# Summing the nine product planes of an image: one strided tensor_reduce in place of four additions

## The chip, the cores and the metric

The kernel runs on one core of one Trainium2 chip. The metric is the device time of one execution in microseconds (us). Three timed runs of the kernel before gave 154.48, 154.02 and 157.14 us, so their median is 154.48 us. All data are fp32.

## The reference, cut to what matters

The input x is 8 images of 32 channels of 128 x 128 points. Two layers follow each other. The first scales and filters each image with a 3 x 3 filter per group of channels, whose nine taps come from the mean of the image through a small matrix, a normalisation and a tanh. The second takes a 2-D Hartley transform, keeps 20 x 20 modes, mixes the channels of each mode with a weight matrix, transforms back, blurs over the images, the channels, the rows and the columns, and sets the columns of high frequency to zero.

```python
lf = tanh(bn(x.mean((2, 3)) @ conv_w.T))            # nine taps per image and group
low = sum(shifted(x, t) * lf[t] for t in range(9))  # reflect padding at the edges
x = (low * (inside + 1) - inside * gap) * lamb_l + x * (lamb_h + 1)
x_ht = dht_2d(x)
out_ht[:, :, :20, :20] = compl_mul2d(x_ht[:, :, :20, :20], w1)
y = gaussian_smoothing_4d(dht_2d(out_ht) / (H * W)) * mask
```

The kernel never filters the full image. It transforms the raw image first and applies the filter to the kept modes: each mode of the filtered image is a sum of nine products (the real and imaginary part of the mode times a coefficient, four for the edge rows and three for the edge columns). That sum of nine is what the change touches.

## The kernel before, in words

**First part, image by image (n = 0 to 7).** SyncE loads an image in four pieces. TensorE transforms the rows of each piece (`stage1(n, g)`, L370), VectorE transposes the result out of PSUM in two halves (`turn_y(n, 0)` and `turn_y(n, 1)`, L715), TensorE transforms the other axis (`stage2(n)`, L385), VectorE transposes that into the tile `data` (`turn_data(n)`, L724). TensorE then computes the filter logits from `data` (`filter_logits`, L399), ScalarE makes the taps (`taps(n)`, L607 and L612), TensorE spreads them (`pick_taps`, L405) and ScalarE copies them (L618), and TensorE multiplies them with a table into coefficients in PSUM (`coefficients(n)`, L418).

**The combination on VectorE, one per image m.** `combine_products(m)` (L736 to L748) multiplies data and coefficients: planes 0 to 5 of the tile `terms`, and a small tile `prod_a`. `combine_edges(m)` sums `prod_a` with a tensor_reduce (L756, 144 elements to 18 per partition) and writes planes 6 to 8 of `terms` (L758). `combine_sum(m)` adds the nine planes of 126 elements per partition (L767 to L773) and writes `parts` (L780), the sums and differences of mode pairs. Each of these steps waits by the semaphore `f_step` for the one before it on the same engine.

**The order on VectorE** is written out by hand. In the pass for n (2 to 7) it is: `combine_products(n - 2)`, `turn_y(n, 0)`, `turn_data(n - 1)`, `combine_edges(n - 2)`, `combine_sum(n - 2)`, `turn_y(n, 1)`. In the pass for n = 7 one more instruction, `share_early` (L787, semaphore `last_share`), comes between `combine_sum(5)` and `turn_y(7, 1)`. After the passes come the combinations of images 6 and 7.

**The order on TensorE** in the same pass: `stage1(n, 0)`, `coefficients(n - 2)`, `stage1(n, 1)`, `stage2(n - 1)`, `stage1(n, 2)`, `filter_logits(n - 1)`, `stage1(n, 3)`, `pick_taps(n - 1)`. `stage2(n - 1)` needs both halves of `turn_y(n - 1, ...)`.

**Behind the passes.** GpSimd blurs over the images as the `parts` come (L897 to L902, tile `acc`). For output images 0 and 1, ScalarE lays `acc` out as the operand `mixin_a` (L590, L630) once `last_share` is there; only then it makes the taps of images 6 and 7, for which TensorE waits. TensorE mixes channels for these two (`mix_early`, L444) between `coefficients(6)`, `stage2(7)`, `filter_logits(7)` and `coefficients(7)`. GpSimd and VectorE lay out `mixin_b` for the other six images (L590, L905), which `mix_late` needs.

**Second part, image by image.** TensorE runs `turn` (L496), `to_columns` (L514) and `to_rows` (L532); ScalarE and VectorE copy between them out of PSUM (L563, L650, L834, L569). SyncE stores the rows of an image in three pieces (L346) as they become ready.

Of the kernel before, what the change touches and what calls it, by code (L numbers as in the profile page):

```python
# [8 lines left out]
MODES = 20  # L9
GROUPS, TAPS = 8, 9  # L10
J, Q, S = 4, 3, 2
# [8 lines left out]
NB1 = MODES + 1  # L20
WIDE = SQ * NB1
ND, NA, NB = 2 * WIDE, 3 * SQ * 8, 4 * WIDE
NTAB = ND + NA + NB
NTERM = 9
# [154 lines left out]
def hartley_conv_kernel(nc, x, wide, taps_table, params, conv_wt, mix_w, out):  # L179
    fp32 = mybir.dt.float32  # L180
    ALU = mybir.AluOpType
    ACT = mybir.ActivationFunctionType
    AX = mybir.AxisListType
# [5 lines left out]
    def view(ap, *dims):  # L189

        return bass.AP(tensor=ap.tensor, offset=ap.offset, ap=[ap.ap[0], *[list(d) for d in dims]])
# [6 lines left out]
    with ctx:  # L198
        def sb(name, shape):
            return ctx.enter_context(nc.sbuf_tensor(name, shape, fp32))  # L200

        def sem(name):
# [15 lines left out]
        prod_a = sb("prod_a", [128, 3 * SQ, 8])  # L218
        coef_a = sb("coef_a", [128, 3 * SQ])
        terms = sb("terms", [128, NTERM, WIDE])  # L220
        parts = sb("parts", [128, 2, 2, Q * MODES])
        spread = sb("spread", [128, N, PLANE])
        acc = sb("acc", [128, N, PLANE])
# [19 lines left out]
        coef_done, coef_used, f_step, parts_done, spread_done, acc_done, last_share = map(  # L243
            sem, ("coef_done", "coef_used", "f_step", "parts_done", "spread_done", "acc_done", "last_share"))
# [10 lines left out]
        B_T, B_F = 3, (5, 6, 7)  # L255
        B_IDLE = 3
        B_TURN, B_MIX_A, B_MIX_B = 1, 0, (0, 7, 0)
        F_LINKS = 7
        WPART = S * Q * MODES // 8

        def const(offset, *dims):
# [425 lines left out]
        def _(dve):  # L687
            tt, tr = nc.vector.tensor_tensor, nc.vector.tensor_reduce
# [63 lines left out]
            def combine_edges(m):  # L752

                base = m * F_LINKS
                dve.wait_ge(f_step, base + 1)
# [5 lines left out]
            def combine_sum(m):  # L761

                base = m * F_LINKS
                flat = lambda plane, count: view(terms[:, plane, 0:1], (1, count * WIDE))
                dve.wait_ge(coef_used, m + 1)
                dve.wait_ge(f_step, base + 3)
                tt(flat(0, 4), flat(0, 4), flat(4, 4), ALU.add).then_inc(f_step, 1)  # L767
                dve.wait_ge(f_step, base + 4)
                tt(flat(0, 2), flat(0, 2), flat(2, 2), ALU.add).then_inc(f_step, 1)
                dve.wait_ge(f_step, base + 5)  # L770
                tt(flat(0, 1), flat(0, 1), flat(1, 1), ALU.add).then_inc(f_step, 1)
                dve.wait_ge(f_step, base + 6)
                tt(flat(0, 1), flat(0, 1), flat(8, 1), ALU.add).then_inc(f_step, 1)  # L773
                dve.wait_ge(f_step, base + 7)
                if m >= 2:
                    dve.wait_ge(acc_done, m - 1)
                low = view(terms[:, 0, 0:1], (NB1, Q), (1, MODES))
                high = view(terms[:, 0, Q * NB1 + MODES:Q * NB1 + MODES + 1], (NB1, Q), (-1, MODES))
                for part, op in ((0, ALU.subtract), (1, ALU.add)):
                    last = tt(view(parts[:, m % 2, part, 0:1], (MODES, Q), (1, MODES)), low, high, op)  # L780
                last.then_inc(parts_done, 1)
# [12 lines left out]
            for n in range(1, N):  # L794
                if n >= 2:
                    combine_products(n - 2)
                turn_y(n, 0)
                turn_data(n - 1)
                if n == 2:
                    dve.wait_ge(basis_in, 16)  # L800
                if n >= 2:
                    combine_edges(n - 2)
                    combine_sum(n - 2)
                if n == N - 1:
                    share_early()
                turn_y(n, 1)
# [5 lines left out]
            last.then_inc(gaps_zero, 1)  # L812
            combine_edges(N - 2)
            combine_sum(N - 2)
            combine_products(N - 1)
            combine_edges(N - 1)
            combine_sum(N - 1)

            dve.wait_ge(parts_done, N)
# [151 lines left out]
```

## Time and profile before

| | us |
|---|---|
| median of three runs | 154.48 |
| the profiled execution: its own time | 155.25 |
| its span, first to last instruction | 153.4 |
| TensorE busy | 132.0 (86%) |
| VectorE busy | 84.7 (55%) |
| GpSimd busy | 55.1 (36%) |
| ScalarE busy | 34.0 (22%) |
| mean granted TensorE clock, share of full speed | 0.929 |

A row of the profile names the line of the kernel, the engine, the operation, the tile written and the tile read, and the shape as partitions x elements per partition. An idle time stands with what ended it, its releaser. The time around the span (155.25 less 153.4, so 1.85 us) is not resolved in the trace. Busy shares are averages over stages that have different limits, so a stage has to be read by itself.

### The profile page before, as it was taken

The page shows a single profiled execution, that of the slowest core. Times are in us where ns is not written, and L with a number is a line of the kernel's source. Part 1 is how long each engine was busy: PE and PEld are TensorE (multiplying, and loading weights), DVE is VectorE, ACT ScalarE, POOL GpSimd, SP SyncE. Part 2 cuts the span into 40 slices and gives each one's busy share as a digit, 9 for nine tenths or more (in the row PEclk, how much of TensorE's full clock was granted, in tenths as well). Part 3 has the DMA queues.
Part 4 walks back from the last instruction along what each step waited for, and adds up shares of the span by engine and source line. Part 5 has one row for each costly group of instructions (what it writes and reads, how often), then busy time and mean ns, then how long its engine had stood idle before and what let it go on. Part 6 is the DMA issues. An engine that isn't in the chain of part 4 may idle for free.

```text
span 153.4 us, 5617 instructions
## 1 busy us (share of the span) xinstructions
PE 132.0 (86%) x2508; PEld 76.8 (50%) x2508; DVE 84.7 (55%) x188; ACT 34.0 (22%) x86; POOL 55.1 (36%) x40
## 2 busy tenths in 40 slices
PE   6656999999999999950999999889999999999700
PEld 4322454545454545420566856745785766746200
DVE  0033347899989898993028994045536345454400
ACT  3000310202020202008003353123334342343300
POOL 8999400040737281919999571000000000000000
PEclk9995599999999999996559999999999999999985
DMA  4999999999999997000000006906955988989993
GB/s 145 310 238 299 353 351 355 366 365 366 365 351 361 349 349 230 0 0 0 4 4 4 6 4 218 326 12 222 328 210 196 364 301 284 383 287 386 378 385 140
DMA packets 35456, 36.79 MB, mean 240 GB/s; under 512 B 1156, under 2 KB 35284, under 8 KB 35432
## 3 DMA queue, kind: packets, MB, share of 16 engines
q1 hardware_dynamic: 35432, 36.43, 71.8%
q8 instruction: 20, 0.33, 0.9%
q14 instruction: 4, 0.03, 0.1%
HBM read 19.65 MB, written 16.78 MB: 238 GB/s over the span
## 4 chain that ended last, share of the span: by engine, by line
PE 78%; DMA 6%; DVE 4%; SPq 3%; ACT 2%; issue 2%; ACTq 0%; DVEq 0%
PE ps L532 19%; PE ps L370 18%; PE ps L385 11%; PE ps L514 8%; PE ps L496 7%; DMA x_ring<-x 6%; PE ps L418 6%; PE ps L444 5%; PE ps L405 1%; SPq L312 1%; ACT mixin_a L590 1%; PE ps L357 1%; PE ps L399 1%; DVE rows L569 1%; DVE data L724 1%
## 5 line engine op out<-in xcount | busy, mean ns | idle before, releaser
L370 PE MATMUL ps<-x_ring,k_wide 64*64 64x256 f32 x512 | 38.5, 426 | 4.5 <-DMA x_ring<-x 4.5
L532 PE MATMUL ps<-cols,k_wide 128*64 128x330 f32 (+1 forms) x192 | 31.4, 467 | 0.1
L370 PEld LDWEIGHTS ps<-x_ring,k_wide 64*64 64x64 f32 x512 | 18.4, 145 | 20.8 <-issue 11.0
L715 DVE STREAM_TRANSPOSE y_sb<-ps 128x1024 f32<-128x1024 f32 x16 | 19.9, 1242 | 15.6 <-PE ps L370 15.6
L532 PEld LDWEIGHTS ps<-cols,k_wide 128*64 128x64 f32 x192 | 12.7, 136 | 13.5 <-issue 5.4
L569 DVE COPY rows<-ps 128x330 f32<-128x330 f32 (+1 forms) x24 | 12.6, 525 | 10.2 <-PE ps L532 9.4
L385 PE MATMUL ps<-y_sb,k_wide 128*32 128x256 f32 x256 | 17.1, 411 | 0.0
L900 POOL TENSOR_TENSOR spread<-parts,k_wide 128x960 f32<-128x960 f32 (+1 forms) x5 | 8.6, 1728 | 18.8 <-DVE parts L780 18.8
L569 ACT COPY rows<-ps 128x330 f32<-128x330 f32 (+1 forms) x24 | 11.1, 462 | 18.0 <-PE ps L532 18.0
L514 PEld LDWEIGHTS ps<-k_wide,modes 64*64 64x64 f32 x384 | 11.8, 134 | 3.9 <-issue 3.6
L514 PE MATMUL ps<-k_wide,modes 64*64 64x66 f32 x384 | 12.9, 220 | 0.0
L385 PEld LDWEIGHTS ps<-y_sb,k_wide 128*32 128x32 f32 x256 | 8.4, 118 | 7.8 <-issue 4.1
L607 ACT ACTIVATE tap_tanh<-ps,bn 72x1 f32<-72x1 f32 x8 | 2.8, 348 | 42.3 <-PE ps L399 42.3
L902 POOL TENSOR_TENSOR acc<-acc,spread 128x960 f32<-128x960 f32 (+1 forms) x5 | 10.7, 2132 | 0.4
L496 PE MATMUL ps<-k_wide,mixed 96*32 96x96 f32 (+2 forms) x512 | 10.5, 233 | 0.0
L496 PEld LDWEIGHTS ps<-k_wide,mixed 96*32 96x32 f32 x512 | 9.7, 109 | 1.7 <-issue 1.3
L418 PE MATMUL ps<-table,kb 10*32 10x396 f32 (+1 forms) x128 | 9.4, 599 | 0.0
L834 DVE COPY cols<-ps 128x396 f32<-128x396 f32 x7 | 4.0, 571 | 9.6 <-PE ps L514 9.6
L724 DVE STREAM_TRANSPOSE data<-ps 128x512 f32<-128x512 f32 x8 | 5.7, 717 | 4.8 <-PE ps L385 4.8
L405 PE MATMUL ps<-tap_scaled,par 74*64 74x32 f32 x16 | 2.5, 242 | 5.6 <-ACT tap_scaled L612 5.6
L897 POOL TENSOR_TENSOR acc<-parts,k_wide 128x960 f32<-128x960 f32 x1 | 1.8, 1789 | 14.9 <-DVE parts L780 14.9
L563 ACT COPY modes<-ps 128x384 f32<-128x384 f32 (+1 forms) x10 | 4.6, 482 | 11.4 <-PE ps L496 11.4
(62 smaller groups left out, 130.9 us busy)
## 6 DMA issues: line engine op xcount, KB each, us to landing
x_ring<-x SPq DMA_DIRECT2D x32, 512.0 KB, 8.9
out<-rows SPq DMA_DIRECT2D x16, 640.0 KB, 4.4
out<-rows SPq DMA_DIRECT2D x8, 768.0 KB, 5.0
w_sb<-mix_w SPq DMA_DIRECT2D x8, 240.0 KB, 8.2
k_wide<-wide SPq DMA_DIRECT2D x1, 328.0 KB, 8.3
k_wide<-wide SPq DMA_DIRECT2D x1, 224.0 KB, 9.8
table<-taps_table SPq DMA_DIRECT2D x2, 78.8 KB
k_wide<-wide SPq DMA_DIRECT2D x1, 128.0 KB, 2.2
```

Source lines behind the costliest of these rows:

```text
L370: last = nc.tensor.matmul(ps[side * 64:side * 64 + 64, g // 2 * 2 + odd, g % 2 * size:(g % 2 + 1) * size], k_wide[half, O_LT + r * YC:O_LT ...
L385: last = nc.tensor.matmul(ps[32 * j:32 * j + 32, B_DATA, part * C * IDX:(part + 1) * C * IDX], const(O_RU + (part * 2 + side) * FN, (1, FN ...
L418: last = nc.tensor.matmul(ps[32 * j:32 * j + 32, B_COEF + part, 0:size], kb[rows_in, n % 2, :], table[rows_in, j * NROW:j * NROW + size], ...
L444: last = nc.tensor.matmul(view(ps[q * C:(q + 1) * C, bank, at:at + 1], (1, 2 * J * count)), w_sb[:, (s * Q + q) * MODES + b, :], mixin[:, ...
L496: last = nc.tensor.matmul(ps[32 * quad:32 * quad + 32, B_TURN + bank, slot * C:slot * C + size], mixed[:, n, s * J + j, :], k_wide[0:Q * C ...
L514: last = nc.tensor.matmul(ps[half, B_T + t // 6, (t % 6) * NW:(t % 6 + 1) * NW], modes[half, u, first * NF:first * NF + 64], k_wide[half, ...
L532: last = nc.tensor.matmul(ps[64 * g:64 * g + 64, row_bank(n, k), 0:nt * NW], const(O_LH + s * H + r * H // 2, (1, H // 2)), cols[:, u, 6 * ...
L569: return copy(view(rows[:, n % 2, s, r, 0:1], (3 * 2 * H, nt), (H - HALF, 2), (1, HALF)), view(ps[:, row_bank(n, k), 0:1], (NW, nt), (HALF ...
L715: nc.vector.transpose(view(y_sb[:, n % 2, unit * half, 0, 0:1], (1, half * YC)), view(ps[:, 2 * unit, 0:1], (1, half * YC))).then_inc(y_re ...
L724: nc.vector.transpose(view(data[:, n % 2, 0, 0, 0:1], (FN, 2), (2 * FN, IDX), (1, FN)), view(ps[:, B_DATA, 0:1], (C * IDX, 2), (1, IDX), ( ...
L900: tt(spread[:, lo:, :], src, weight, ALU.mult).then_inc(spread_done, 1)
L902: tt(acc[:, lo:, :], acc[:, lo:, :], spread[:, lo:, :], ALU.add).then_inc(acc_done, 1)
```

## The change

A tile `total` of 126 elements per partition is added. `combine_sum` sums the nine planes with one tensor_reduce, which reads `terms` in the order: element i of plane 0, of plane 1, ..., of plane 8, then element i + 1. The nine values of one sum lie 126 elements, so 504 bytes, apart. The four additions and three of the waits between them go. `parts` is computed from `total` and no longer from plane 0 of `terms`. `F_LINKS`, the count of `f_step` per image, follows.

```diff
+        total = sb("total", [128, WIDE])
...
-        F_LINKS = 7
+        F_LINKS = 4
...
             def combine_sum(m):
 
                 base = m * F_LINKS
-                flat = lambda plane, count: view(terms[:, plane, 0:1], (1, count * WIDE))
                 dve.wait_ge(coef_used, m + 1)
                 dve.wait_ge(f_step, base + 3)
-                tt(flat(0, 4), flat(0, 4), flat(4, 4), ALU.add).then_inc(f_step, 1)
+                tr(total[:, :], view(terms[:, 0, 0:1], (1, WIDE), (WIDE, NTERM)), AX.X, ALU.add).then_inc(f_step, 1)
                 dve.wait_ge(f_step, base + 4)
-                tt(flat(0, 2), flat(0, 2), flat(2, 2), ALU.add).then_inc(f_step, 1)
-                dve.wait_ge(f_step, base + 5)
-                tt(flat(0, 1), flat(0, 1), flat(1, 1), ALU.add).then_inc(f_step, 1)
-                dve.wait_ge(f_step, base + 6)
-                tt(flat(0, 1), flat(0, 1), flat(8, 1), ALU.add).then_inc(f_step, 1)
-                dve.wait_ge(f_step, base + 7)
                 if m >= 2:
                     dve.wait_ge(acc_done, m - 1)
-                low = view(terms[:, 0, 0:1], (NB1, Q), (1, MODES))
-                high = view(terms[:, 0, Q * NB1 + MODES:Q * NB1 + MODES + 1], (NB1, Q), (-1, MODES))
+                low = view(total[:, 0:1], (NB1, Q), (1, MODES))
+                high = view(total[:, Q * NB1 + MODES:Q * NB1 + MODES + 1], (NB1, Q), (-1, MODES))
```

## Rows read from the trace of the kernel before

**Rows 1.** Chain that ended last: start us, us, what; one pass, then the hand-over.

```profile
55.81 1.86 PE ps L385 x32
...
63.22 1.91 PE ps L385 x32
...
65.15 0.72 DVE data L724
...
66.74 0.69 DVE terms L767
...
68.56 0.04 DVE parts L780
...
69.31 0.49 ACT mixin_a L590
```

**Rows 2.** Waits of PE: engine line waited for, us in total, times, longest.

```profile
PE ps L405 <- ACT tap_scaled L612: 5.6, 1, 5.6
```

**Rows 3.** VectorE in order of time: start, us, line, operation, [idle before], around pass 7.

```profile
61.42 1.24 DVE L715 STREAM_TRANSPOSE y_sb<-ps 128x1024 f32<-128x1024 f32 x1
65.15 0.72 DVE L724 STREAM_TRANSPOSE data<-ps 128x512 f32<-128x512 f32 x1 [0.16 <-PE ps L385]
```

**Rows 4.** Tiles terms and prod_a: ns min/median/max, first and last start, forms.

```profile
L758 DVE TENSOR_TENSOR terms<-coef_a,k_wide x8: 553/553/1176, 29.0 to 87.5; 128x378 f32<-128x378 f32 x8
L767 DVE TENSOR_TENSOR terms<-terms x8: 683/683/1118, 29.7 to 88.2; 128x504 f32<-128x504 f32 x8
L769 DVE TENSOR_TENSOR terms<-terms x8: 420/420/422, 30.4 to 88.9; 128x252 f32<-128x252 f32 x8
L771 DVE TENSOR_TENSOR terms<-terms x8: 291/291/292, 30.9 to 89.4; 128x126 f32<-128x126 f32 x8
...
L736 DVE TENSOR_TENSOR prod_a<-data,ps x8: 191/192/230, 25.2 to 86.0; 128x72 f32<-128x72 f32 x8
L738 DVE TENSOR_TENSOR prod_a<-data,ps x8: 216/216/223, 25.4 to 86.2; 128x72 f32<-128x72 f32 x8
L756 DVE TENSOR_REDUCE coef_a<-prod_a x8: 258/260/296, 28.7 to 87.2; 128x18 f32<-128x144 f32 x8
```

**Rows 5.** VectorE by line and form: busy us, mean ns; the patterns with far steps.

```profile
L563 DVE COPY modes<-ps 128x288 f32<-128x288 f32 x6 | 2.7, 458 | 4.1 <-PE ps L496 4.1
L590 DVE COPY mixin_b<-parts 32x120 f32<-32x120 f32 x4 | 1.1, 284 | 0.1
L575 DVE COPY mixed<-ps 96x256 f32<-96x256 f32 x1 | 0.4, 421 | 4.6 <-PE ps L444 4.6
```

**Rows 6.** TensorE and GpSimd in order of time, as rows 3, behind the passes.

```profile
77.22 3.42 PE L385 MATMUL ps<-y_sb,k_wide 128*32 128x256 f32 x31
...
95.46 3.60 PE L444 MATMUL ps<-mixin_b,w_sb 128*32 128x64 f32 x180
100.14 1.37 PE L444 MATMUL ps<-mixin_b,w_sb 128*32 128x64 f32 x60 [1.08 <-issue]
...
90.50 1.93 POOL L905 TENSOR_SCALAR mixin_b<-parts 32x60 f32<-32x60 f32 x4 [0.43 <-DVE parts L780]
```

**Rows 7.** Stretches: us, busy of PE, PEld, DVE, ACT, POOL, granted clock, DMA share, GB/s.

```profile
15.00:62.00 47.00, 47.00 (x712) 22.55 (x712) 38.86 (x87) 6.57 (x20) 16.41 (x9) 0.96 1.04 342
12.00:13.00 1.00, 0.89 (x8) 0.55 (x12) 0.00 (x0) 0.00 (x0) 1.00 (x1) 0.50 1.06 245
18.00:19.00 1.00, 1.00 (x16) 0.27 (x12) 0.27 (x1) 0.00 (x0) 0.00 (x0) 0.58 1.08 356
70.00:70.10 0.10, 0.00 (x0) 0.00 (x0) 0.10 (x1) 0.09 (x2) 0.10 (x1) 0.65 0.00 0
80.20:80.30 0.10, 0.10 (x8) 0.10 (x1) 0.00 (x0) 0.00 (x0) 0.10 (x1) 0.65 0.00 0
135.00:137.00 2.00, 2.00 (x16) 0.98 (x14) 0.96 (x2) 0.73 (x2) 0.00 (x0) 1.00 0.60 201
137.00:139.00 2.00, 2.00 (x48) 1.38 (x46) 0.57 (x1) 0.93 (x3) 0.00 (x0) 1.00 1.07 381
```

## The prediction

> **What bounds the kernel now.** I read the chain of waits first, for the work that sets the end, then the stretches, to see whether that work is ever idle, then VectorE in order of time, because the change lies there alone.
>
> In the passes over the images TensorE sets the pace. In the chain, stage2 begins at 55.81 in one pass and at 63.22 in the next, so a pass takes 7.41 us [rows 1], and over the 47 us from 15 to 62 TensorE is busy for 47.00 us [rows 7]. VectorE follows close behind. The second half of turn_y, which stands behind the sum in VectorE's order, runs from 61.42 to 62.66 [rows 3], and stage2 takes it up at 63.22 [rows 1]: 0.56 us to spare. At the data transpose VectorE waits 0.16 us for stage2 [rows 3]. That 0.16 us is the whole slack of VectorE's round per pass: a round longer by more than that slows the loop, and a shorter one gives TensorE nothing.
>
> The loop ends in a hand-over that does cross VectorE. After pass 7 TensorE stops for 5.6 us until the taps of image 6 are there [rows 2]. The chain runs through data at 65.15, the first addition of image 5 at 66.74, parts at 68.56, share_early, and ScalarE's mixin_a from 69.31 [rows 1]. ScalarE makes the taps only behind mixin_a, so every nanosecond of the sum of image 5 counts. The sums of images 6 and 7 come later and are covered, as shown below.
>
> **The change part by part.** *Removed, per image:* four additions of 683, 420, 291 and 291 ns at the median [rows 4]; with their waits, the stretch from the first addition to parts is 68.56 - 66.74 = 1.82 us [rows 1]. The waits are thus 1.82 - 1.685 = 0.14 us, some 34 ns after each of the four.
>
> *Added:* one tensor_reduce over 9 x 126 = 1134 elements. The nearest row is the tensor_reduce of this kernel, 144 elements in 260 ns. The additions give the slope: (683 - 420) / 252 = 1.044 ns per element [rows 4]. So 260 + 990 x 1.044 = 1294 ns, 1.29 us, and 1.33 us with its wait. Gain per image 1.82 - 1.33 = 0.49 us.
>
> What the trace does not show is a VectorE read from SBUF in which every element lies 504 bytes from the last. **Lower end:** if the fixed part of the reduce were as large as that of an addition (420 - 252 x 1.044 = 157 ns), its 144 elements would cost 0.72 ns each, and the new one would take 0.97 us. **Upper end:** prod_a is made by two products of 72 elements; the one that reads runs of 2 takes 216 ns, the one with runs of 4 takes 192 [rows 4]. If the 24 ns were the price of 18 further runs, 1.33 ns each, the reduce, in which each element is a run, would take 1.29 + 1.51 = 2.80 us. But the first kind reached 230 ns too [rows 4], so the 24 ns may be mere overlap with the instruction ahead. I take 1.29 us, because the far steps that the trace does show on VectorE cost nothing: modes reads PSUM in steps of 128 bytes, 288 elements in 458 ns; mixed in steps of 256 bytes, 256 in 421 ns; mixin_b writes SBUF in steps of 384 bytes, 120 in 284 ns [rows 5]. The slope and the fixed part of the additions give 458, 424 and 282.
>
> Against it stands a rule of the Trainium skill, "SBUF — State Buffer", section "Door 1: The DMA port swizzle": consecutive accesses within a 16-byte line of SBUF go at full rate, and an access to a new line pays a penalty, so fp32 may be stepped over 4 elements for free. Here each access would be to a new line. It gives no size, the three rows above do not bear it out, and no row here shows the very case. By the skill the sum would turn from a gain into a loss.
>
> *In the loop (images 0 to 4):* the gain of 0.49 us per pass is worth nothing, because TensorE's 7.41 us cover it; VectorE waits 0.65 us for stage2 where it waited 0.16. GpSimd starts its blur step 0.49 us sooner, which nothing waits for. Without the cover, that is if VectorE set the loop, the five would be worth 2.45 us.
>
> *At the hand-over (image 5):* 0.49 us off the chain. ScalarE starts at about 68.8 and TensorE idles 5.06 us. Nothing of other engines is named as a releaser between data and mixin_a [rows 1], so no other wait is next in line within 0.49 us that I can see.
>
> *The clock takes some of it back.* The granted clock fell from full speed to half (2.4 to 1.2 GHz) at 70.03 and rose at 80.27 [rows 7]; TensorE had stopped before the fall, and was at work again well before the rise. If the rise moves with the work, all 0.49 us stay. If it stays where it is in time, 0.49 us more of stage2(7) runs slow: it took 3.42 us there [rows 6] against 1.91 at full speed [rows 1], so 0.49 x 1.91 / 3.42 = 0.27 us is gained. I take the middle, 0.38, rounded 0.4 us.
>
> *After the hand-over (images 6 and 7):* two shorter sums, worth nothing. mix_late starts at 95.46 behind TensorE's own work; its last input, GpSimd's mixin_b, is ready at 90.50 + 1.93 = 92.43 [rows 6], 3.0 us earlier. In one of the eight images the first addition took 1118 and not 683 ns [rows 4]; if that is one of these two, its sum gains 0.4 us more, off the path. Should the cover go, they would be worth about a microsecond. The stores do not set the end before the last image: from 135 to 137 the DMA engines were busy 0.60 of the time [rows 7], so they still waited for rows, and an earlier TensorE ends the kernel earlier by the same amount.
>
> *The new tile, F_LINKS, the read of parts from total:* no instruction more, same form and size; 0.
>
> **Sum:** -0.4 us. The profiled execution took 155.25 us (span 153.4 and 1.85 around it) and would take 154.85; it lies 0.77 us above the median of the three runs, 154.48, from which I forecast 154.1 us.
>
> **The rivals.**
>
> *The strided read is slow, and the kernel slower.* Place: the reduce of each pass, ahead of turn_y(n, 1). It decides from where the round outgrows the slack: reduce + 0.04 > 1.82 + 0.16, so from 1.94 us on. The fixed part of the reduce is 260 - 144 x 1.044 = 110 ns, so with two stream steps per element it would take 0.11 + 1134 x 2 x 1.044 / 1000 = 2.48 us: five passes lose 2.52 - 1.98 = 0.54 us each and the hand-over 0.70, together 3.4 us, 157.9 us. At the upper end of 2.80 us: 5 x 0.86 + 1.02 = 5.3, 159.8 us. For it: the 216 against 192 ns. Against it: [rows 5].
>
> *The clock turns a small shift into a large one.* One slow stretch ran from 12.0 to about 18.8 (0.58 in the slice from 18 to 19), 6.8 us, the other 10.2 us [rows 7]. One that is 3.4 us shorter or longer is worth 3.4 x (1 - 0.56) = 1.5 us: 152.6 or 155.6 us. Against it: 0.49 us is small beside the stretch. For it: the three runs differ by 3.1 us for the same kernel.
>
> *VectorE sets the loop after all.* All six sums count: 6 x 0.49 = 2.9 us, 151.5 us. Against it: the 47.00 of 47 us and the 0.16 us in which VectorE waits.
>
> *The end does not move.* A fetch or another stall, like the 1.08 us in which TensorE waited for nothing that the trace names before its last 60 matmuls of mix_late [rows 6], eats the 0.4 us: 154.5 us. It could go away or double as well, which keeps the range at a microsecond on either side.
>
> **How the numbers follow.** Forecast 0.68; slow read 0.12; clock 0.10; end unmoved 0.07; VectorE's loop 0.03. The range is 153.0 to 156.0 us: below, the stall gone; above, the longer slow stretch and the 0.77 us by which an execution may stand above the median. It leaves out the slow read, the loop case and a part of the clock case, 0.19 in all. A measurement tells 2% (3.1 us) from no change. Slower by more: the slow read, most of its 0.12, so 0.10. Faster by more: 0.02, a loop gain with the clock on top. Within 2%: 0.88.
>
> **What the changed profile would show.** A tensor_reduce of 1134 elements to 126 at about 1.29 us, the same with and without GpSimd at work; VectorE's wait for stage2 at 0.65 us per pass; a pass still 7.41 us; TensorE's wait for the taps at 5.1 us; 24 fewer instructions on VectorE. I am wrong if the reduce exceeds 1.94 us, if the pass changes, or if mixin_a does not start about 0.5 us earlier relative to the data transpose.

## The result, and the profile after

The changed kernel is slower: median 156.84 us (155.36 to 158.86, six runs) against 154.68 us for the kernel before in the same session (six runs). The ratio is 1.0136, 95% interval 1.0089 to 1.0183, so 1.4 to 2.8 us more. The forecast was 154.1 us, range 153.0 to 156.0. The sign was wrong and the median lies above the range. A second timing in a later session gave 156.63 against 155.64 us, ratio 1.0112 (1.0016 to 1.0208), so about 1.7 us more. The medians are those of all runs, while the ratios leave out the runs in which a kernel fell into a slower state (7 of the 17 of the kernel before in the later session), so differences are read from the ratios.

The profiled execution of the first session, 158.86 us (span 157.1), was the longest of its six, with two stalls of TensorE in the second part (1.1 us in all) that the second profile does not have. So the places in time are read from the second profile of the same kernel, span 155.7 us. In both, the reduce and the passes are the same.

The tile `terms` of the changed kernel (first profile), columns as in [rows 4]:

```profile
L745 DVE TENSOR_TENSOR terms<-data,ps x8: 399/402/410, 25.7 to 88.0; 128x252 f32<-128x252 f32 x8
L749 DVE TENSOR_TENSOR terms<-data,ps x8: 662/666/672, 26.1 to 88.4; 128x504 f32<-128x504 f32 x8
L759 DVE TENSOR_TENSOR terms<-coef_a,k_wide x8: 552/553/1389, 29.3 to 89.3; 128x378 f32<-128x378 f32 x8
L767 DVE TENSOR_REDUCE total<-terms x8: 2264/2270/2308, 29.9 to 89.9; 128x126 f32<-128x1134 f32 x8
```

The reduce takes 2.27 us, not 1.29. With its wait the sum takes 2.31 us where the four additions took 1.82 [rows 1, 4]: 0.49 us longer, the very amount by which it was to be shorter. It also stands beside GpSimd's work (2308 ns at most) almost unmoved, while L759 goes up to 1389.

The first and last stage2 of the passes in the kernel before (start us, us, line, operation):

```profile
26.09 1.93 PE L385 MATMUL ps<-y_sb,k_wide 128*32 128x256 f32 x32
...
63.15 1.93 PE L385 MATMUL ps<-y_sb,k_wide 128*32 128x256 f32 x32
```

The beginnings of stage2 in the second profile of the changed kernel, and the end of TensorE's wait for the taps:

```profile
26.35 1.93 PE L386 MATMUL ps<-y_sb,k_wide 128*32 128x256 f32 x32
...
33.81 1.93 PE L386 MATMUL ps<-y_sb,k_wide 128*32 128x256 f32 x32
...
41.42 1.93 PE L386 MATMUL ps<-y_sb,k_wide 128*32 128x256 f32 x32
...
56.65 1.93 PE L386 MATMUL ps<-y_sb,k_wide 128*32 128x256 f32 x32
...
64.27 1.93 PE L386 MATMUL ps<-y_sb,k_wide 128*32 128x256 f32 x32
...
74.64 0.42 PE L406 MATMUL ps<-tap_scaled,par 74*64 74x32 f32 x2 [6.08 <-ACT tap_scaled L613]
```

A pass takes 7.61 or 7.62 us from the second on, where it took 7.41 [rows 1]; the first one still fits in 7.46. From 26.35 to 64.27 it is 37.92 us. TensorE's wait for the taps is 6.08 us in place of 5.6 [rows 2].

VectorE in one pass of the second profile, in order of time:

```profile
57.69 1.23 DVE L716 STREAM_TRANSPOSE y_sb<-ps 128x1024 f32<-128x1024 f32 x1
58.85 0.67 DVE L725 STREAM_TRANSPOSE data<-ps 128x512 f32<-128x512 f32 x1
59.44 0.26 DVE L757 TENSOR_REDUCE coef_a<-prod_a 128x18 f32<-128x144 f32 x1
59.74 0.55 DVE L759 TENSOR_TENSOR terms<-coef_a,k_wide 128x378 f32<-128x378 f32 x1
60.39 2.28 DVE L767 TENSOR_REDUCE total<-terms 128x126 f32<-128x1134 f32 x1
62.70 0.35 DVE L774 TENSOR_TENSOR parts<-total 128x60 f32<-128x60 f32 x2
62.97 1.24 DVE L716 STREAM_TRANSPOSE y_sb<-ps 128x1024 f32<-128x1024 f32 x1
```

The wait of 0.16 us ahead of the data transpose [rows 3] is gone; the transpose begins while the one before it is ending. VectorE has become the engine that sets the passes. The chain of waits of this profile says the same: in the passes it used to run through TensorE alone, and now it runs through VectorE alone (first the reduce, then the transpose that stands behind it):

```profile
60.39 2.29 DVE total L767
...
63.05 0.29 DVE y_sb L716
...
65.39 1.16 DVE y_sb L716
...
68.01 2.28 DVE total L767
...
71.06 0.48 ACT mixin_a L591
```

So the trace accounts for this. Passes: 37.92 us against 37.06 in the profile before (26.09 to 63.15), 0.86 us. Hand-over, from the last stage2 in the passes to mixin_a: 71.06 - 64.27 = 6.79 against 69.31 - 63.15 = 6.16, 0.63 us (the order of time puts the last stage2 of before at 63.15, the chain that counts from its release at 63.22 [rows 1]). Together 1.49 us, 0.96% of the time, which lies inside both intervals (in the first one only just).

### The profile page after: what moved, and what is told of

It reads as the page before. It is cut to its first block, busy times and chain, and to the rows that moved or that the text cites. A ratio compares the mean times of both kernels' runs of the same rounds, so it can differ in the third digit from the quotient of the medians.

```text
span 157.1 us, 5593 instructions
## 1 busy us (share of the span) xinstructions
PE 132.6 (84%) x2508; PEld 76.3 (49%) x2508; DVE 88.6 (56%) x164; ACT 34.0 (22%) x86; POOL 54.7 (35%) x40
## 4 chain that ended last, share of the span: by engine, by line
PE 53%; DVE 25%; issue 6%; DMA 6%; SPq 3%; ACT 2%; DVEq 0%; ACTq 0%
PE ps L533 19%; DVE total L767 9%; PE ps L515 8%; PE ps L497 7%; DMA x_ring<-x 6%; PE ps L445 5%; PE ps L386 5%; PE ps L371 5%; DVE y_sb L716 5%; PE ps L419 2%; DVE data L725 2%; DVE terms L759 2%; DVE terms L749 2%; DVE terms L745 1%; SPq L313 1%
## 5 line engine op out<-in xcount | busy, mean ns | idle before, releaser
L371 PE MATMUL ps<-x_ring,k_wide 64*64 64x256 f32 x512 | 37.3, 412 | 5.0 <-DMA x_ring<-x 5.0
L371 PEld LDWEIGHTS ps<-x_ring,k_wide 64*64 64x64 f32 x512 | 17.5, 140 | 21.0 <-issue 10.0
L767 DVE TENSOR_REDUCE total<-terms 128x126 f32<-128x1134 f32 x8 | 18.2, 2277 | 0.8
L386 PE MATMUL ps<-y_sb,k_wide 128*32 128x256 f32 x256 | 17.8, 424 | 0.1
L497 PE MATMUL ps<-k_wide,mixed 96*32 96x96 f32 (+2 forms) x512 | 11.0, 233 | 1.1 <-issue 1.1
```

The costliest lines, as they stand in the source:

```text
L371: last = nc.tensor.matmul(ps[side * 64:side * 64 + 64, g // 2 * 2 + odd, g % 2 * size:(g % 2 + 1) * size], k_wide[half, O_LT + r * YC:O_LT ...
L386: last = nc.tensor.matmul(ps[32 * j:32 * j + 32, B_DATA, part * C * IDX:(part + 1) * C * IDX], const(O_RU + (part * 2 + side) * FN, (1, FN ...
L497: last = nc.tensor.matmul(ps[32 * quad:32 * quad + 32, B_TURN + bank, slot * C:slot * C + size], mixed[:, n, s * J + j, :], k_wide[0:Q * C ...
L767: tr(total[:, :], view(terms[:, 0, 0:1], (1, WIDE), (WIDE, NTERM)), AX.X, ALU.add).then_inc(f_step, 1)
```

## The experiments

Times are medians of each kernel's runs and of the kernel before on the same chip; the ratio, with its 95% interval, is the one reported with them, and a difference in us is the ratio's, worked out on the median of the kernel before. Traces are read in segments: the passes from the stage2 of image 1 to that of image 6, and from there to mixin_a.

| kernel | us (runs) | before, us (runs) | ratio (95%) | passes, hand-over against before, us |
|---|---|---|---|---|
| products side by side | 154.47 (12) | 154.71 (29) | 1.0015 (0.9977 to 1.0052) | +0.06, -0.06 |
| reduce for images 0 to 4 | 155.47 (6) | 154.71 (29) | 1.0102 (1.0032 to 1.0171) | +0.68, +0.16 |
| reduce for image 5 | 155.24 (12) | 154.71 (29) | 1.0049 (1.0006 to 1.0091) | +0.26, +0.47 |
| reduce for images 6, 7 | 155.08 (12) | 154.71 (29) | 1.0055 (1.0016 to 1.0094) | +0.07, +0.01 |
| changed kernel again | 156.63 (6) | 155.64 (17) | 1.0112 (1.0016 to 1.0208) | +0.86, +0.63 |
| filler and four additions | 157.66 (6) | 155.64 (17) | 1.0185 (1.0095 to 1.0276) | +0.94, +0.65 |
| taps of image 6 first | 154.70 (12) | 155.64 (17) | 0.9923 (0.9867 to 0.9978) | see below |
| planes 128 apart | 156.61 (6) | 155.76 (17) | 1.0159 (1.0058 to 1.0260) | +0.17, +0.38 |
| side by side, taps first | 153.78 (12) | 155.76 (17) | 0.9947 (0.9898 to 0.9997) | see below |

In three of these traces TensorE waited for an image within the passes: 0.76 us (images 0 to 4), 1.30 us (image 5), 0.56 us (images 6, 7). Those waits are taken out of the column. They cannot be taken out cleanly, since VectorE catches up in them: the +0.26 of the kernel with the reduce for image 5 alone, whose passes are otherwise those of before, shows the error.

**1. The products side by side.** Is it the far step, or the reduce itself?

```diff
-        terms = sb("terms", [128, NTERM, WIDE])
+        terms = sb("terms", [128, WIDE, NTERM])
...
-tr(total[:, :], view(terms[:, 0, 0:1], (1, WIDE), (WIDE, NTERM)), AX.X, ALU.add)
+tr(total[:, :], view(terms[:, 0, 0:1], (NTERM, WIDE), (1, NTERM)), AX.X, ALU.add)
```

The three product steps write with an innermost step of NTERM elements, 36 bytes.

> The nine products of one sum are laid side by side in terms (36 bytes per sum), so the reduce reads 1134 adjacent elements; the three product steps write in steps of 36 bytes instead. Theory A (VectorE reads SBUF slowly where each element lies far from the last): the reduce falls from 2.27 us to 1.29 us, the products stay at 402, 666 and 553 ns, a pass is back at 7.41 us, and the kernel takes 0.4 us less than the kernel before, 154.1 to 154.3 us. Theory B (a tensor_reduce with many short sums is slow in any layout): the reduce stays at about 2.27 us and the kernel at 156 to 157 us. A third case: the writes in steps of 36 bytes are slow, and the products gain what the reduce loses.

```profile
L745 DVE TENSOR_TENSOR terms<-data,ps x8: 601/606/616, 26.5 to 86.7; 128x252 f32<-128x252 f32 x8
L749 DVE TENSOR_TENSOR terms<-data,ps x8: 1077/1108/1120, 27.0 to 87.1; 128x504 f32<-128x504 f32 x8
L759 DVE TENSOR_TENSOR terms<-coef_a,k_wide x8: 843/848/1361, 30.1 to 88.3; 128x378 f32<-128x378 f32 x8
L768 DVE TENSOR_REDUCE total<-terms x8: 1333/1334/1336, 31.0 to 89.3; 128x126 f32<-128x1134 f32 x8
```

The reduce of adjacent elements takes 1.33 us: my price of 1.29 was right for it, and theory B falls. But the third case came true: the writes cost what the reads no longer do. 606 for 402, 1108 for 666 and 848 for 553 ns are 0.81, 0.88 and 0.78 ns more per element written; the far reads had cost (2270 - 1334) / 1134 = 0.83 ns per element read. Someone has to take the far step, and the time of the kernel is that of the kernel before. By their durations the products take 0.94 us longer. In VectorE's round it is 0.78 us, because a step that follows without a wait starts up to 0.16 us before the end of the one ahead (1.40 us in place of 0.92 from L745 to the transpose behind it, 0.95 in place of 0.65 from L759 to the sum). Less the 0.45 us by which the sum is shorter, the round is 0.3 us longer than before. That is about the slack worked out below, and the last passes take 7.44 us.

**2. The reduce at one place at a time.** The four additions stay for the other images; REDUCED is (0, 1, 2, 3, 4), (5,) or (6, 7).

```diff
+        REDUCED = (0, 1, 2, 3, 4)
...
+                if m in REDUCED:
+                    tr(total[:, :], view(terms[:, 0, 0:1], (1, WIDE), (WIDE, NTERM)), AX.X, ALU.add).then_inc(f_step, 1)
...
+                else:
+                    tt(flat(0, 4), flat(0, 4), flat(4, 4), ALU.add).then_inc(f_step, 1)
```

Images 0 to 4:

> The strided tensor_reduce for images 0 to 4 only, the four additions for images 5, 6 and 7. Theory A (the round of VectorE sets the passes): a pass takes 7.61 us in place of 7.41, and the kernel takes 5 x 0.2 = 1.0 us more than the kernel before. Rival (the passes hide it, the loss comes elsewhere): no difference.

```profile
31.13 1.93 PE L390 MATMUL ps<-y_sb,k_wide 128*32 128x256 f32 x32
38.75 1.93 PE L390 MATMUL ps<-y_sb,k_wide 128*32 128x256 f32 x32
```

Its passes without a late image take 7.47, 7.62, 7.46 and 7.61 us; the two short ones are the first and the one behind the late image. By the ratio it takes 1.6 us more (0.5 to 2.6). The passes do lose. The rival, that they hide it, falls.

Image 5:

> The strided tensor_reduce for image 5 only, the one whose sum stands before the hand-over from the passes to the mixing. If the cost lies on the path: 2.31 us for the sum in place of 1.82, so TensorE's wait for the taps is 6.1 us in place of 5.6 and the kernel takes 0.3 to 0.5 us more. Rival: a change of the clock makes it 1.5 us more or less.

```profile
PE ps L410 <- ACT tap_scaled L617: 6.0, 1, 6.0
```

The wait went from 5.6 to 6.0 us, and the kernel takes 0.8 us more by the ratio (0.1 to 1.4). The expected 0.3 to 0.5 us lies within that.

Images 6 and 7:

> The strided tensor_reduce for images 6 and 7 only, behind the hand-over. If these sums are covered (mix_late starts 3 us after its last input): no difference within 0.3 us. Rival: VectorE gets late for the rows, modes or columns that follow, or mixin_b for mix_late, and TensorE shows a wait there: 0.5 to 1.1 us more.

The trace shows no new wait of TensorE. GpSimd's last part of mixin_b, the last input of mix_late, is later by less than the cover:

```profile
90.18 1.93 POOL L916 TENSOR_SCALAR mixin_b<-parts 32x60 f32<-32x60 f32 x4 [1.25 <-DVE parts L791]
```

It ends at 92.11, and mix_late begins at 94.99 in this trace. Yet by the ratio it takes 0.9 us more, and the interval (0.2 to 1.5 us) leaves out zero. The expectation of at most 0.3 us is neither kept nor clearly missed. From mixin_a to the last rows, less the stalls without a releaser, its trace takes 74.7 us where the kernel before takes 74.4. But the trace of images 0 to 4 takes 74.7 us too, with the four additions for images 6 and 7. In both, the stretch at half clock began 2.3 us after mixin_a and not 0.7, and stage2(7) took 3.65 us in place of 3.42 [rows 6]. So these 0.3 us are not shown to come from the two sums, and the rest no trace shows.

**3. The changed kernel again.** No edit.

> The changed kernel itself once more, on the chip of the next three. From its trace: five passes at 0.2 us more each, 0.45 us more at the hand-over, so 1.4 to 1.6 us more than the kernel before. If the 2.1 us of the first timing come back, something beyond these two places costs about 0.6 us.

1.7 us by the ratio (0.2 to 3.2), 1.49 us in the trace. The expectation is kept. The interval is too wide to say whether the 2.1 us of the first timing returned.

**4. A filler of the same length.** Does the far read harm anyone else, or is only VectorE's time lost?

```diff
+                first = view(terms[:, 0, 0:1], (1, 290))
+                tt(filler[:, :], first, first, ALU.add).then_inc(f_step, 1)
+                dve.wait_ge(f_step, base + 4)
                 tt(flat(0, 4), flat(0, 4), flat(4, 4), ALU.add).then_inc(f_step, 1)
```

> The kernel before with its four additions, and ahead of them one more addition over 290 elements into a scratch tile that nobody reads: 290 x 1.044 + 157 = 0.46 us and 0.03 us of wait, as much as the strided reduce is longer than the four additions. Theory (what costs is only the time that VectorE's sum takes): passes of 7.61 us, the wait for the taps 6.1 us, and the same 1.4 to 2.1 us more as the changed kernel. Rival (the strided read does harm to others, by its traffic in SBUF): passes below 7.61 us and less than half of the loss.

```profile
33.31 1.93 PE L386 MATMUL ps<-y_sb,k_wide 128*32 128x256 f32 x32
40.94 1.93 PE L386 MATMUL ps<-y_sb,k_wide 128*32 128x256 f32 x32
...
63.84 1.93 PE L386 MATMUL ps<-y_sb,k_wide 128*32 128x256 f32 x32
```

Passes of 7.63 us and 1.59 us in the two segments, with every read near. In these two segments the loss is at least that of the changed kernel: VectorE's time alone explains it, and the rival falls. The whole kernel takes 2.9 us more (1.5 to 4.3), above the changed one. In this trace the stretch at half clock behind the hand-over lasted 13.7 us (69.9 to 83.6) and not 10.2 [rows 7], and the stall in mix_late 1.73 and not 1.08 us [rows 6].

**5. Single steps of VectorE, alone.** 23 steps behind the last rows of the changed kernel, each waiting for the one before: a reduce of 9 x 126 at innermost steps of 1, 2, 3, 4, 8, 32, 126, 127 and 128 elements (L883 to L899); reduces of 4 x 126 far and near, from SBUF and from PSUM (L901 to L907); additions with no, one or two far reads and a far write (L909 to L915); copies from SBUF near, far read, far write (L917 to L921), and from PSUM (L923 to L927).

```diff
+                tr(probed[:, 0:126], src((1, 126), (4, 9)), AX.X, ALU.add).then_inc(probe_ready, 1)
+                steps += 1; dve.wait_ge(probe_ready, steps)
...
+                tt(dst((4, 126), (1, 4)), src((1, 126), (126, 4)), src((4, 126), (1, 4)), ALU.add).then_inc(probe_ready, 1)
```

> The changed kernel with 23 single steps of VectorE behind its last rows, each three times and each waiting for the one before, so nothing else runs beside them. Theory A (every access far from the last costs extra, in SBUF, on either side): a reduce of 9 x 126 takes 1.33 us at steps of 1, and 2.27 us at 126, 127 and 128 elements alike; additions and copies of 504 elements take 0.4 us more with a far read or a far write; from PSUM no extra. Rival 1 (banks of SBUF): 126, 127 and 128 elements differ. Rival 2 (reduce only): additions and copies show no extra. Where the extra begins (2, 3, 4, 8 or 32 elements) is open; the kernel's time means nothing here.

By line, mean ns of three (the fourth number behind the shapes):

```profile
L895 DVE TENSOR_REDUCE probed<-probe 128x126 f32<-128x1134 f32 x3 | 6.8, 2264 | 0.1
L897 DVE TENSOR_REDUCE probed<-probe 128x126 f32<-128x1134 f32 x3 | 6.5, 2177 | 0.1
L891 DVE TENSOR_REDUCE probed<-probe 128x126 f32<-128x1134 f32 x3 | 6.5, 2163 | 0.1
L889 DVE TENSOR_REDUCE probed<-probe 128x126 f32<-128x1134 f32 x3 | 6.5, 2162 | 0.1
L893 DVE TENSOR_REDUCE probed<-probe 128x126 f32<-128x1134 f32 x3 | 6.2, 2054 | 0.1
L899 DVE TENSOR_REDUCE probed<-probe 128x126 f32<-128x1134 f32 x3 | 6.2, 2054 | 0.1
L887 DVE TENSOR_REDUCE probed<-probe 128x126 f32<-128x1134 f32 x3 | 5.2, 1740 | 0.1
L883 DVE TENSOR_REDUCE probed<-probe 128x126 f32<-128x1134 f32 x3 | 4.0, 1334 | 0.1
L885 DVE TENSOR_REDUCE probed<-probe 128x126 f32<-128x1134 f32 x3 | 4.0, 1334 | 0.1
L913 DVE TENSOR_TENSOR probed<-probe 128x504 f32<-128x504 f32 x3 | 3.5, 1183 | 0.1
L915 DVE TENSOR_TENSOR probed<-probe 128x504 f32<-128x504 f32 x3 | 3.1, 1025 | 0.1
L911 DVE TENSOR_TENSOR probed<-probe 128x504 f32<-128x504 f32 x3 | 3.1, 1023 | 0.1
L927 DVE COPY probed<-ps 128x504 f32<-128x504 f32 x3 | 3.0, 1011 | 0.1
...
L905 DVE TENSOR_REDUCE probed<-ps 128x126 f32<-128x504 f32 x3 | 2.0, 683 | 0.1
L923 DVE COPY probed<-ps 128x504 f32<-128x504 f32 x3 | 2.0, 683 | 0.1
L925 DVE COPY probed<-ps 128x504 f32<-128x504 f32 x3 | 2.0, 683 | 0.1
L909 DVE TENSOR_TENSOR probed<-probe 128x504 f32<-128x504 f32 x3 | 2.0, 683 | 0.1
L907 DVE TENSOR_REDUCE probed<-ps 128x126 f32<-128x504 f32 x3 | 2.0, 682 | 0.1
...
L921 DVE COPY probed<-probe 128x504 f32<-128x504 f32 x3 | 1.9, 643 | 0.1
L919 DVE COPY probed<-probe 128x504 f32<-128x504 f32 x3 | 1.9, 635 | 0.1
L917 DVE COPY probed<-probe 128x504 f32<-128x504 f32 x3 | 1.3, 424 | 0.1
```

Theory A holds. Steps of 1 and 2 elements cost 1334 ns, 3 cost 1740, 4 and 8 about 2162. It is not the reduce: an addition goes from 683 to 1023 ns with one far read, to 1183 with two, to 1025 with a far write. A far read or write costs a copy within SBUF 0.21 us, half of the 0.4 us expected. A far read of PSUM costs nothing (L905 far and L907 near: 683 and 682; L925 and L923: 683 and 683). Rival 1 has a small part: 126, 127 and 128 elements give 2264, 2177 and 2054 ns, so the exact step matters by a tenth, where the expectation had the three alike.

**6. Planes 128 elements apart.** The fastest of those three steps leaves the sum 0.27 us longer than the additions.

```diff
+PITCH = 128
...
-        terms = sb("terms", [128, NTERM, WIDE])
+        terms = sb("terms", [128, NTERM, PITCH])
```

> The changed kernel with the planes 128 elements apart in place of 126; the edge products are written with the same lengths. The single steps gave 2.05 us for a reduce at 128 and 2.26 us at 126. So the sum takes 2.09 us, 0.27 us more than the four additions. Theory (the passes give way only when VectorE's round grows by more than its slack of 0.29 us): passes at 7.41 us again, only the hand-over 0.27 us longer, so 0.3 us more than the kernel before. Rival (every nanosecond of VectorE counts in the passes): passes of 7.5 us, 0.9 us more.

```profile
L769 DVE TENSOR_REDUCE total<-terms x8: 2069/2124/2223, 28.9 to 88.0; 128x126 f32<-128x1134 f32 x8
```

Within the kernel the reduce took 2124 ns at the median, not 2054, so it stood just at the threshold: passes of 7.41, 7.41, 7.48, 7.46 and 7.47 us, near the theory and clear of the 7.61 of step 126. The trace shows 0.55 us in both segments together. The time does not agree: 2.5 us more by the ratio (0.9 to 4.0). In the trace the stall in mix_late adds another 0.55 us (1.63 for 1.08). The passes are settled by the trace, the time of this kernel is not.

**7. The taps of image 6 first.** The hand-over, not the sum, is where TensorE stands still.

```diff
-            for n in range(N - 2):
+            for n in range(N - 1):
                 taps(n)
...
-            taps(N - 2)
             taps(N - 1)
```

> The kernel before, but ScalarE makes the taps of image 6 before it lays out mixin_a. The wait at the hand-over is then for mixin_a and no longer for mixin_a and the taps behind it: mixin_a ends at about 72.1 us where TensorE went on at 72.9, so 0.5 to 0.8 us less than the kernel before, 153.9 us. Rival: the taps of image 6 wait for a coefficient step or the clock takes it back, no difference.

```profile
PE ps L444 <- ACT mixin_a L630: 4.7, 1, 4.7
```

The wait falls from 5.6 to 4.7 us. The kernel is faster than the one before: 1.2 us by the ratio (0.3 to 2.1). From the last stage2 of the passes to the last rows, less the stalls without a releaser, its trace is 1.7 us shorter, and the wait is only 0.9 of that. The stretch at half clock lasted 6.8 us (71.1 to 77.9) where it lasted 10.2 before [rows 7], and stage2(7) took 2.73 us in place of 3.42 [rows 6]:

```profile
76.27 2.73 PE L385 MATMUL ps<-y_sb,k_wide 128*32 128x256 f32 x31
```

How much of the 1.2 us is the wait and how much the clock the timing cannot tell.

**8. Both.** The layout of experiment 1 with the order of experiment 7.

> The layout with adjacent products together with the taps of image 6 made before mixin_a. The sum at the hand-over is 0.15 us shorter than the four additions (0.45 less for the sum, 0.30 more for the edge products), the passes are 0.03 us longer each. Expected: within 0.3 us of the kernel that only makes the taps first, so 0.9 to 1.3 us less than the kernel before. Rival: the longer products cost in the passes what the sum gains, and it comes out worse than the taps alone by over 0.5 us.

The wait is 4.6 us, and the ratio 0.9947 is no better than 0.9923 of experiment 7 alone: 0.8 us less than the kernel before (0.05 to 1.6), where 0.9 to 1.3 was expected. The two cannot be told apart. Both beat the kernel before and the changed one. The simpler, experiment 7, keeps the four additions.

## Why the prediction was wrong

**The step that failed is the choice of the price of the reduce.** "I take 1.29 us, because the far steps that the trace does show on VectorE cost nothing" rested on three rows [rows 5], and none of them was a witness. Two read PSUM, where experiment 5 shows the far step to be free (683 against 683 ns). The third, mixin_b, does write SBUF at far steps, 120 elements in 284 ns, and I compared it with the 282 ns of an addition. But it is a copy within SBUF, and such a copy goes at nearly twice the rate: 504 elements in 424 ns where the addition takes 683. By an estimate with the fixed part of the additions, 120 elements would take 157 + 120 x (424 - 157) / 504 = 221 ns at that rate, and 273 ns at the rate of the copy with a far write (643 ns for 504). The 284 ns held a penalty that I read as none. The Trainium skill, "VectorE: DVE Perf Modes", section "Mode 2×_2P — use both read ports for one tensor", says that a copy of fp32 within SBUF may move two elements at a time and an addition may not; the trace agrees with 424 and 683 ns.

**The rule set aside was right in kind.** The Trainium skill, "SBUF — State Buffer", section "Door 1: The DMA port swizzle", puts a penalty on each access to a new 16-byte line. Experiment 5 agrees: 2162 against 1334 ns. It differs from the page in where the penalty starts. The page lets fp32 step 4 elements for free; here 3 already cost 406 ns and 4 cost 828 ns, as much as 8, and of these steps only 2 was free. The same passage asks for at least two accesses per line, and that does fit: a step of 2 elements makes two, a step of 4 makes one.

**The bounds held, and the rival was there.** 2.27 us lies between 0.97 and 2.80. "The strided read is slow, and the kernel slower" was the rival, with 0.12, far too little for a page's rule against three rows that were not of the case. Its mechanism came as written: passes first, then the hand-over. Its size did not. It gave 157.9 us at two stream steps per element. The reduce took 2.27 and not 2.48 us, and the slack of VectorE's round was not the 0.16 us of idle time. When the data transpose follows turn_y without a wait, it starts 0.08 us before that ends and takes 0.67 us in place of 0.72 (second profile), so another 0.13 us is gained and the slack is 0.29 us. With it, 0.49 - 0.29 = 0.20 us per pass, which is what 7.61 against 7.41 us shows; by the 0.16 it would have been 0.33. The threshold is then 1.82 + 0.29 - 0.04 = 2.07 us and not 1.94, and experiment 6, at 2.12 us, lost 0.05 to 0.07 us in its last passes.

**The clock** was given 0.4 us of swing for the forecast and its own rival of 1.5 us. From mixin_a to the last rows, less the stalls without a releaser, the traces of the kernel before, the changed one (second profile) and the filler take 74.4, 74.1 and 74.9 us. So the clock took back 0.3 us of the 1.5 in the changed kernel: there the stretch at half clock again lasted 10.2 us (71.2 to 81.5), but it began 0.2 us after mixin_a and not 0.7, and stage2(7) took 3.16 us in place of 3.42. In the filler it lasted 13.7 us, so the longer stretch of the rival did come, and in this trace it cost 0.4 us and not 1.5. Most of the shift passed on to the end.

**The sums of images 6 and 7** have cover by the trace (2.9 us ahead of mix_late). Timed alone they cost 0.9 us (0.2 to 1.5) that this does not explain. The prediction had them at nothing, and whether that is right stays open.

**What stays open:** the times of experiments 2 (images 6 and 7) and 6, which are longer than their traces account for. The two timings of the changed kernel, 2.1 and 1.7 us, both have the 1.5 us of the trace in their intervals, so they do not show that anything is missing there.

## What to carry to other kernels

Count the far steps of an operation, on the read and on the write side, before counting its instructions: here one reduce in place of four additions with near reads would have saved 0.45 us, and it paid 0.94 us for 1134 reads in SBUF at far steps. A row proves the price of an access pattern only if memory, side and kind of operation are the same. An idle time of 0.16 us beside a saturated engine is little cover: the slack was 0.29 us, and of a step longer by 0.49 us the rest showed in every pass. A filler of the suspected length tells in one run whether an engine's time alone costs that.

## What the runs showed of the hardware that was not expected

- VectorE, fp32, SBUF: 1134 elements reduced in 1334 ns at innermost steps of 1 or 2 elements, 1740 at 3, 2162 at 4 and at 8, 2054 to 2264 at 32 to 128. A far write costs as much as a far read (1025 and 1023 ns against 683 for 504 elements), two far reads only half as much again (1183). A far read of PSUM has no price (683 and 683 ns); a PSUM copy that writes SBUF at far steps takes 1011 against 683 ns.
- Beside GpSimd's work a long reduce with one SBUF input was hardly touched by GpSimd (2308 ns at most against 2270), while the product with two, L759, went from 553 to 1389 ns in the same stretch.
- TensorE stalled inside mix_late, ahead of its last 60 matmuls, in all twelve profiles, for 0.9 to 1.7 us, with nothing named as the cause; 1.08 us in [rows 6], 1.38 in the second profile of the changed kernel.
